# Queries and values of batch 0 and keys of batches 0 to 2, projected in the first stage and finished one half per expert block

## The chip, the cores and the metric

One core of one Trainium2 chip. The time is the device time of one execution in microseconds. PE is TensorE, DVE VectorE, ACT ScalarE, POOL GpSimd; SP issues DMAs only.

## The reference

```
xn  = layernorm(x)                       # x (4, 1024, 256), no scale or shift
q   = xn @ Wq + bq  -> 8 heads of 128    # k, v = xn @ Wkv + bkv, one head of 128 for all
q, k += sinusoidal positions             # (1024, 128)
s   = softmax(causal(q @ k.T / sqrt(128))) @ v @ Wo
g   = silu(moe(xn))   # 8 experts, top 2 of a softmax over router logits;
                      # relu(xn @ w1 + b1) @ w2 + b2, 256 -> 1024 -> 256
out = x + s * g
```

## The kernel before

Every matrix product is done in float16 halves: an operand is split into a high half (the value rounded to f16) and a low half (the rest), and three products (high by high, high by low, low by high: `PASSES`) are added in PSUM. So a projection of 128 columns of weights by 512 tokens, called a **job** here, is six matmuls of 512 columns (two chunks of 128 inputs by three passes); a job of values ("V") is 24 matmuls of 128. A query or key of 1024 tokens is two jobs. Each job is finished in steps: scale and add positions (DVE), add the bias and round to the high half (ACT), subtract for the low half (DVE).

**First stage** (`routing`). DVE, ACT and POOL normalise x (32 tiles of 128 rows) and split it; PE turns it; PE multiplies by the router's weights; DVE picks the two experts of each row (`choose`), PE counts (`counts`), DVE works out slots and one-hot rows (`one_hots`), and PE adds up, in eight groups of 8 matmuls (`place`), which token stands in each of 71 units of 128 rows. With that table (`who`) POOL gathers rows. POOL also splits the key/value weights and, of Wq, head 0 alone (L809 to L815). PE projects K and Q of head 0 of batch 0, four jobs (`project`, L482); ACT copies their banks to SBUF (L606), and one DMA puts them into DRAM (`kq_d`). ACT and DVE also split the weights of experts 0 and 1.

**Expert stage** (`experts`). 40 blocks, in the order `ORDER`: 22 of two units of 128 rows (twins), then 9 twins in turn with 9 of one unit. PE does `up` of block n between `down` of block n-1. Each block has four quarters q: ACT does the ReLU of quarter q (L1008) out of PSUM, DVE splits it (`split`: L1032 and L1034), PE's `down` of the next block's time reads it. DVE's `rows(n-2)` (L1044) stands between the splits of quarters 0 and 1. Behind the fourth ReLU, ACT's queue issues the transposing loads of block n+3 (L218), the store of the outputs of block n-2 (L996) and reads the next block's expert number. POOL gathers one unit and splits one piece of weights (512 columns) at a time (L261 to L265): experts 2 to 7, then Wq (4 pieces), then Wo (4 pieces); SP issues the loads. In blocks 30, 32, 34 and 36 (`KQ_AT`) one of the four early jobs is finished in a **round**: positions (L1061, DVE, behind the split of quarter 0), high half (L1014, ACT, behind the fourth ReLU), low half (L1065, DVE, in the next block behind the split of quarter 0).

**Attention** (`attention`). 32 heads n of five groups of score rows. PE does scores, values of the head before, and jobs given by the table `Jobs`: for step k = 5n+i the job that PE projects there.

```
if n == 0:
    job = (("Q", 1, 0), ("Q", 1, 1), ("V", 0, 0), ("V", 0, 1), ("Q", 2, 0))[i]
...
elif i in (0, 2) and n + 2 < heads:
    job = ("Q", n + 2, i // 2)
elif i == 1 and n % HEADS >= 4 and HEADS * (b + 1) < heads:
    job, bank = ("KKVV"[n % HEADS - 4], b + 1, n % 2), "S"
```

From head 9 on, the output tile of an earlier batch (`o_tile`, 24 matmuls of 256 columns) comes behind the fifth group. SP turns the probabilities by transposing DMAs (L1571).

## Time and profile before

| what | us |
| --- | --- |
| median of 3 runs (1076.97 to 1078.37) | 1077.34 |
| the profiled execution, its span | 1078.8 |
| PE busy / DVE busy / ACT busy / POOL busy | 990.9 / 857.8 / 641.9 / 336.8 |
| first matmul of the first expert block | 85.12 |
| end of the expert stage | 470.1 |
| first exponential of head 0 | 474.37 |

The profile gives the profiled execution's span and no other time of it, so the span stands for it. "Busy" is the time in which an engine has an instruction in it. In a timeline, a row is one or several instructions in a sequence: its start, its length, engine, source line, what it writes and reads, shapes, and in brackets the idle time of the engine before it and what ended it. ACTq is ACT's instruction queue: a DMA issue is in the queue and not on the engine. "<-issue" is idle time in which the engine waits for its own queue.

### The profile page before, as it was taken

How to read it: one execution, taken by the hardware profiler on the slowest of the kernel's cores; microseconds unless marked ns; L12 is line 12 of the kernel's file. 1: busy time of each engine (PE TensorE's matmuls, PEld its weight loads, DVE VectorE, ACT ScalarE, POOL GpSimd, SP SyncE). 2: the span in 40 equal slices, each digit the busy share in tenths (PEclk: the TensorE clock that was granted, in tenths of full speed). 3: DMA queues.
4: the chain of work that ended last, by engine and by line, in shares of the span. 5: the costliest groups of instructions: out<-in, count | busy, mean ns of one | idle time of the engine just before them, and what ended most of it. 6: DMA issues, size and time to landing. Idle time of an engine off the chain costs nothing.

```text
span 1078.8 us, 25081 instructions
## 1 busy us (share of the span) xinstructions
PE 990.9 (92%) x8686; PEld 778.5 (72%) x8686; DVE 857.8 (80%) x1535; ACT 641.9 (59%) x1358; POOL 336.8 (31%) x350
## 2 busy tenths in 40 slices
PE   0747999999999999998989889999999999999997
PEld 0536888888888898865656667767777677677776
DVE  6985776666766455569999999998999999999971
ACT  2722333233333333357888888878888878788860
POOL 3215999989995000020101002121212111112111
PEclk9968999999999999999999999999999999999999
DMA  8778666666666322149887879798999878888992
GB/s 273 211 287 182 157 181 177 174 179 184 171 172 147 95 60 65 46 121 159 171 154 141 157 142 186 152 164 150 172 189 178 150 150 162 153 171 160 181 179 95
DMA packets 410137, 172.58 MB, mean 160 GB/s; under 512 B 351994, under 2 KB 399940, under 8 KB 409252
## 3 DMA queue, kind: packets, MB, share of 16 engines
q1 hardware_dynamic: 352816, 129.80, 57.5%
q10 hardware_dynamic: 50724, 23.50, 8.6%
q0 software_dynamic: 6480, 17.70, 6.5%
q8 instruction: 77, 1.26, 0.5%
q14 instruction: 40, 0.33, 0.1%
HBM read 52.84 MB, written 31.72 MB: 78 GB/s over the span
## 4 chain that ended last, share of the span: by engine, by line
PE 37%; DVE 10%; DMA 5%; ACT 2%; issue 1%; SPq 0%; ACTq 0%; DVEq 0%
PE b_psO L1265 11%; PE b_psS L1242 11%; PE b_psJ L1281 5%; DMA b_pT<-b_ph 5%; PE b_psJ L1201 5%; DVE b_nmax L1426 3%; DVE b_ph L1462 3%; PE b_psS L1292 2%; PE b_psO L1267 1%; PE b_psS L1201 1%; DVE b_outs L1468 1%; ACT b_pr L1346 1%; ACT b_ph L1376 1%; PE b_psS L1245 1%; DVE b_Q L1449 1%
## 5 line engine op out<-in xcount | busy, mean ns | idle before, releaser
L933 PE MATMUL psU<-bxT,w_p 128*128 128x256 f16 (+1 forms) x1920 | 287.5, 262 | 13.3 <-DVE w_p L276 9.3
L1008 ACT ACTIVATE h<-psU,bias 128x256 f32<-128x256 f32 (+1 forms) x320 | 125.3, 448 | 273.6 <-PE psU L933 171.5
L942 PE MATMUL psY<-w_p,hp 128*128 x1704 | 273.4, 273 | 2.1 <-DVE hp L1034 2.1
L1242 PE MATMUL b_psS<-b_kp,b_Q 128*128 128x512 f16 (+3 forms) x1152 | 218.8, 326 | 1.5 <-PEq L1086 1.5
L1346 ACT ACTIVATE b_pr<-b_psS,b_nmax 128x1024 f32<-128x1024 f32 (+7 forms) x256 | 187.0, 735 | 47.9 <-DVE b_nmax L1426 27.1
L933 PEld LDWEIGHTS psU<-bxT,w_p 128*128 x1920 | 188.4, 98 | 34.0 <-issue 15.1
L1265 PE MATMUL b_psO<-b_pT,b_vp 128*128 128x256 f16 x1536 | 189.7, 274 | 20.3 <-issue 13.5
L1462 DVE SCALAR_TENSOR_TENSOR b_ph<-b_pr,b_rrec,b_ph 128x1024 f16<-128x1024 f32 (+7 forms) x256 | 199.4, 810 | 0.0
L1376 ACT ACTIVATE b_ph<-b_pr,b_rrec 128x1024 f16<-128x1024 f32 (+7 forms) x256 | 187.0, 768 | 15.4 <-DVE b_rrec L1455 14.1
L1032 DVE CAST hp<-h 128x512 f16<-128x512 f32 (+1 forms) x160 | 88.9, 556 | 133.7 <-ACT h L1008 127.5
L1426 DVE TENSOR_REDUCE b_nmax<-b_psS 128x1 f32<-128x1024 f32 (+7 forms) x256 | 183.1, 746 | 13.9 <-PE b_psS L1245 12.4
L942 PEld LDWEIGHTS psY<-w_p,hp 128*128 128x128 f16 x1704 | 166.1, 98 | 23.4 <-issue 3.5
L1265 PEld LDWEIGHTS b_psO<-b_pT,b_vp 128*128 128x128 f16 x1536 | 145.0, 98 | 44.1 <-issue 19.1
L1242 PEld LDWEIGHTS b_psS<-b_kp,b_Q 128*128 128x128 f16 x1152 | 103.2, 98 | 78.9 <-issue 2.2
L1539 POOL DMA_INDIRECT b_yg<-expert_outputs,pos x64 | 68.4, 1069 | 246.1 <-DMA expert_outputs<-y 119.5
L1545 POOL TENSOR_TENSOR b_x_row<-b_G,b_x_row 128x256 f32<-128x256 f32 x24 | 17.4, 727 | 368.6 <-DVE b_G L1489 359.8
L1034 DVE TENSOR_TENSOR hp<-h,hp 128x512 f16<-128x512 f32 (+1 forms) x160 | 127.1, 794 | 5.5
L179 POOL DMA_INDIRECT rowx<-xn_split,who x71 | 78.0, 1099 | 65.9 <-DVE who L796 43.4
L1281 PE MATMUL b_psJ<-b_wo,b_outs 128*128 128x256 f16 x576 | 66.9, 273 | 0.0
L265 POOL TENSOR_TENSOR w_p<-wstage,w_p 128x512 f16<-128x512 f32 x48 | 64.5, 1343 | 4.1
L1366 ACT ACTIVATE b_Q<-b_psJ,bias 128x512 f16<-128x512 f32 x59 | 40.6, 687 | 32.5 <-DVE b_psJ L1435 32.1
L1281 PEld LDWEIGHTS b_psJ<-b_wo,b_outs 128*128 128x128 f16 x576 | 55.2, 98 | 6.5
(187 smaller groups left out, 1027.1 us busy)
## 6 DMA issues: line engine op xcount, KB each, us to landing
wstage<-in_L_ffn_w SPq DMA_DIRECT2D x48, 256.0 KB
expert_rows<-rowx SPq DMA_DIRECT2D x67, 128.0 KB
expert_outputs<-y ACTq DMA_DIRECT2D x31, 256.0 KB
a_x_all<-in_L_attn_x SPq DMA_DIRECT2D x8, 512.0 KB, 9.7
...
```

The lines of the kernel that those rows point to most:

```text
L933: mm = eng.matmul(psU[w % U][:, g % 2, 0:tiles * P].rearrange("p (t r) -> p t r", t=tiles), weight(n, a * W1 + c * H + g * P, P), bxT[n % ...
L942: mm = eng.matmul(psY[n % 2][:, t, :], hp[n % 2][:, a, g, t * P:(t + 1) * P], weight(n, 2 * W1 + (2 * g + b) * D, D), start=(g == 0 and k ...
L1008: a = eng.activation(h32[w % 4][:, g, 0:rows], psU[w % U][:, g, 0:rows], ACT.Relu, bias=bias[:, ds(e * HT + 2 * q + g, 1)], scale=1.0 / WS)
L1032: eng.tensor_copy(hi, full).then_inc(hh_, 1)
L1034: eng.tensor_tensor(lo, full, hi, ALU.subtract).then_inc(hl_, 1)
L1242: mm = eng.matmul(dst, Q[n % 3][:, a, u * P:(u + 1) * P], kb[:, c, lo:lo + w], start=(kk == 0), stop=(kk == 2 and not last))
L1265: eng.matmul(both, vb[:, a, j, :], pT[:, at:at + hop + 1:hop, :], start=(j == 0 and kk == 0), stop=False)
L1281: mm = eng.matmul(psJ[:, 0:D], outs[b % many][:, a, h, t * P:(t + 1) * P], wo_p[:, e, h, :], start=(h == 0 and kk == 0), stop=(h == HEADS ...
L1346: a = eng.activation(pr[k % 3][:, o:o + w], psS[BUF[i]][:, :, :].rearrange("p a n -> p (a n)")[:, o:o + w], ACT.Exp, bias=nmax[:, at:at + ...
L1376: a = eng.activation(ph[k % 4][:, 2 * o:2 * o + w], pr[k % 3][:, o:o + w], ACT.Copy, scale=rrec[:, at:at + 1])
L1426: a = eng.tensor_reduce(nmax[:, at:at + 1], psS[BUF[i]][:, :, :].rearrange("p a n -> p (a n)")[:, o:o + w], AX.X, ALU.max, negate=True)
L1462: a = eng.scalar_tensor_tensor(ph[k % 4][:, 2 * o + w:2 * o + 2 * w], pr[k % 3][:, o:o + w], rrec[:, at:at + 1], ph[k % 4][:, 2 * o:2 * o ...
```

## The change

20 jobs more are projected in the first stage, 24 in all (`EARLY`: K0, Q0, V0, Q1 to Q7 of batch 0, K1, K2), two halves j of 512 tokens each; they are taken out of the table of attention. For that, POOL splits the whole of Wq in the first stage (it had come as four pieces in the expert stage), PE projects two jobs between the transposes, four ahead of `counts`, five behind it, one behind each of the first five groups of `place` and eight behind the last, in six PSUM banks; ACT copies each bank to SBUF. All of PE's and ACT's queues wait for the last copy ahead of block 0. In blocks 0 to 7 ACT's queue stores three raw jobs each to DRAM. In blocks 4 to 27 one job per block is finished, as round r = n - 4 (rounds 0 to 7 take jobs 16 to 23, rounds 8 to 23 jobs 0 to 15): positions behind DVE's third split, high behind ACT's fourth ReLU, the store of the halves of round r-1 and the load of round r+1 behind it, low half behind DVE's first split of the next block. The two jobs of V0 (rounds 12 and 13) have no positions. SP loads K0, Q0, V0 and Q1 at the end of its expert part; Q2 to Q7, K1 and K2 are loaded in attention, one per head.

The diff, cut to its core:

```diff
+EARLY = [("K", 0), ("Q", 0), ("V", 0)] + [("Q", h) for h in range(1, HEADS)] + [("K", 1), ("K", 2)]
+EARLY_JOBS = [(kind, m, j) for kind, m in EARLY for j in range(2)]
+NJ = len(EARLY_JOBS)
+JOBS_UP = 16
+ROUND_JOB = list(range(JOBS_UP, NJ)) + list(range(JOBS_UP))
...
-            if job:
+            if job and job not in EARLY_JOBS:
...
+            if e in (3, 4):
+                project(e - 3)
...
-        for r in range(3):
-            project(r)
+        for q in range(2, 6):
+            project(q)
         eng.wait_ge(s_bz, 3)
         counts()
-        project(3)
+        for q in range(6, 11):
+            project(q)
         for s in range(CHUNKS):
             place(s)
-        eng.wait_ge(s_kc, 4)
+            if s < 5:
+                project(11 + s)
+        for q in range(JOBS_UP, NJ):
+            project(q)
+        eng.wait_ge(kqc_, NJ)
...
         eng.wait_ge(xs_, 64)
-        for r in range(4):
-            eng.wait_ge(s_kp, r + 1)
-            eng.activation(kq_f[:, r, :], flat[r], ACT.Copy, scale=SC / WS).then_inc(s_kc, 1)
+        for q in range(NJ):
+            if q == JOBS_UP:
+                eng.wait_ge(s_sp, 1)
+            eng.wait_ge(s_kp, q + 1)
+            eng.activation(v["job_at"][q], job_bank[q % 6], ACT.Copy,
+                           scale=(1.0 if EARLY_JOBS[q][0] == "V" else SC) / WS).then_inc(kqc_, 1)
...
-        for i, (full, p) in enumerate(((wkv_f, wkv_p), (wq_f, wq_p))):
+        for i, (full, p) in enumerate(((wkv_f, wkv_p), (wq_f[:, :, 0:512], wq_h[:, :, :, 0:512]),
+                                       (wq_f[:, :, 512:], wq_h[:, :, :, 512:]))):
...
-        eng.dma_start(wq_f[:, :, :], wq[:, 0:HD].rearrange("(c p) n -> p c n", p=P)).then_inc(s_kw, 16)
+        eng.dma_start(wq_f[:, :, :], wq.rearrange("(c p) n -> p c n", p=P)).then_inc(s_qw, 16)
...
+        def load_raw(r):
+            eng.wait_ge(kqr_[r // 8], 128)
+            if r >= 2:
+                eng.wait_ge(kqb_, r - 1)
+            eng.dma_start(kq_t[r % 2][:, :], kq_d[ROUND_JOB[r]]).then_inc(kql_[r % 2], 16)
+
+        def high(r):
+            if r >= 2:
+                eng.wait_ge(kqs_[r % 2], 16 * (r // 2))
+            if EARLY_JOBS[ROUND_JOB[r]][0] == "V":
+                eng.wait_ge(kql_[r % 2], 16 * (r // 2 + 1))
+                eng.activation(kq_o[r % 2][:, 0], kq_t[r % 2][:, :], ACT.Copy).then_inc(kqa_, 1)
+            else:
+                eng.wait_ge(kqt_, summed(r))
+                eng.activation(kq_o[r % 2][:, 0], kq_t[r % 2][:, :], ACT.Identity, bias=column(r)).then_inc(kqa_, 1)
...
                 a.then_inc(rl_, 1)
-            if n in KQ_AT:
-                r = KQ_AT[n]
-                eng.wait_ge(kqt_, r + 1)
-                eng.activation(kq(r)[0][:, 0], kq_t[:, :], ACT.Identity, bias=kq(r)[1]).then_inc(kqa_, 1)
+            r = n - ROUND0
+            if 0 <= r < NJ:
+                high(r)
+            if 1 <= r <= NJ:
+                put_halves(r - 1)
+            if -1 <= r < NJ - 1:
+                load_raw(r + 1)
+            for i in range(PUT * n, min(PUT * n + PUT, NJ)):
+                put_raw(i)
             if n == 0:
                 v["load"](eng, 2)
...
+        def positions(r):
+            kind, m, j = EARLY_JOBS[ROUND_JOB[r]]
+            if kind != "V":
+                eng.wait_ge(v["pe_"], 16)
+                eng.wait_ge(kql_[r % 2], 16 * (r // 2 + 1))
+                eng.tensor_tensor(kq_t[r % 2][:, :], kq_t[r % 2][:, :], pe_sb[:, j * 512:(j + 1) * 512], ALU.add).then_inc(kqt_, 1)
...
                 split(n, q)
...
+                if q == 0 and 1 <= n - ROUND0 <= NJ:
+                    lower(n - ROUND0 - 1)
+                if q == 2 and 0 <= n - ROUND0 < NJ:
+                    positions(n - ROUND0)
```

**Where the order changes.** PE in the first stage, from the last logits to the first expert block, before (L489 is a projection, L511 a group of placing, L499 to L505 the counts):

```order
L476 MATMUL psU<-a_rw_p,a_xT 128x8 x48
L489 MATMUL psU<-xTb_next,wkv_p 128x512 x12
L489 MATMUL psU<-xTb_next,a_wq_p 128x512 x6
L499 MATMUL psU<-a_one_100,a_M_109 128x128 x2
L504 MATMUL psU<-a_tri_92,a_tot_93 128x264 x2
L505 MATMUL psU<-a_M_109,a_up_99 128x256
L489 MATMUL psU<-xTb_next,a_wq_p 128x512 x6
L511 MATMUL psU<-a_oh_q,a_oh_r 128x71 x64
L885 TENSOR_LOAD blk_e
```

and in the change (L508 and L504 are projections, L530 placing, L518 to L524 the counts):

```order
L523 MATMUL psU<-a_tri_98,a_tot_99 128x264 x2
L524 MATMUL psU<-a_M_115,a_up_105 128x256
L508 MATMUL psY<-xTb_next,wq_late 128x512 x12
L508 MATMUL psU<-xTb_next,wq_late 128x512 x18
L530 MATMUL psU<-a_oh_q,a_oh_r 128x71 x8
L508 MATMUL psU<-xTb_next,wq_late 128x512 x6
...
L530 MATMUL psU<-a_oh_q,a_oh_r 128x71 x24
L508 MATMUL psU<-xTb_next,wq_late 128x512 x12
L508 MATMUL psY<-xTb_next,wq_late 128x512 x12
L508 MATMUL psU<-a_xT,wkv_p 128x512 x24
L921 TENSOR_LOAD blk_e
```

Eight projections now stand between the last group of placing and block 0. ACT from the last ReLU of a block to the first of the next, in the expert stage, before:

```order
L1008 ACTIVATE h_3_132<-psU,bias 128x256
L218 DMA_TRANSPOSE bxT_67<-expert_rows 128x4x128 x2
L996 DMA expert_outputs<-y_72 128x2x256
L885 TENSOR_LOAD blk_e
L885 ISA x2
L1008 ISA
L1008 ACTIVATE h_0_129<-psU,bias 128x256
```

and in the change, in block 6:

```order
L1072 ACTIVATE h_3_137<-psU,bias 128x256
L1054 ACTIVATE kq_o_82<-kq_t_80,bias 128x512
L1059 DMA early_halves<-kq_o_83 256x1x512
L1044 DMA kq_t_81<-early_raw 128x512
L1038 DMA early_raw<-a_jobs_up 128x512 x3
L234 DMA_TRANSPOSE bxT_67<-expert_rows 128x4x128 x2
L1035 DMA expert_outputs<-y_72 128x2x256
L921 TENSOR_LOAD blk_e
L921 ISA x2
L1072 ISA
L1072 ACTIVATE h_0_134<-psU,bias 128x256
```

The high half (L1054) and its wait stand ahead of all that was behind the fourth ReLU. DVE in the change, one block of that kind (L1122 is positions, L1130 the low half):

```order
L1101 CAST hp_138<-h_2_136 128x512
L1103 TENSOR_TENSOR hp_138<-h_2_136,hp_138 128x512
L1122 TENSOR_TENSOR kq_t_80<-kq_t_80,pe_sb 128x512
L1101 CAST hp_138<-h_3_137 128x512
L1103 TENSOR_TENSOR hp_138<-h_3_137,hp_138 128x512
L1101 CAST hp_139<-h_0_134 128x512
L1103 TENSOR_TENSOR hp_139<-h_0_134,hp_139 128x512
L1130 SCALAR_TENSOR_TENSOR kq_o_82<-kq_t_80,bias,kq_o_82 128x512
L921 TENSOR_LOAD blk_e
```

Positions came in behind the third split, and the low half behind the first split of the block after.

## Rows read from the trace of the kernel before

**Rows 1.** Windows, by stage: length, busy us of each engine, granted clock, DMA share, GB/s
```profile
48.00:85.12 37.12, 17.47 (x98) 10.67 (x95) 33.69 (x89) 12.88 (x25) 5.91 (x6) 0.67 0.79 284
...
140.00:320.00 180.00, 180.00 (x1652) 161.33 (x1650) 122.13 (x154) 56.99 (x136) 164.69 (x172) 1.00 0.64 176
320.00:378.00 58.00, 55.83 (x569) 49.63 (x567) 31.10 (x59) 19.61 (x54) 19.21 (x21) 1.00 0.50 123
```

**Rows 2.** Windows of attention heads: 0, 1 to 5, 10, 12 and 13, 30
```profile
474.37:489.46 15.09, 14.58 (x122) 8.86 (x119) 14.25 (x26) 14.03 (x30) 4.67 (x5) 1.00 0.74 184
489.46:579.22 89.76, 78.82 (x598) 53.06 (x598) 85.72 (x153) 75.17 (x155) 9.47 (x10) 1.00 0.85 157
651.11:668.53 17.42, 17.42 (x141) 12.60 (x140) 16.69 (x31) 14.87 (x30) 2.99 (x3) 1.00 0.87 172
685.95:724.25 38.30, 38.30 (x295) 26.49 (x294) 35.77 (x65) 31.11 (x63) 5.89 (x6) 1.00 0.85 152
1013.88:1029.73 15.85, 15.50 (x136) 11.82 (x133) 14.34 (x27) 13.53 (x29) 2.95 (x3) 1.00 0.96 186
```

**Rows 3.** Timeline of PE, first stage: start, us, engine, line, shapes, idle before it
```profile
51.87 1.46 PE L489 MATMUL psU<-xTb_next,a_wq_p 128*128 128x512 f16 x6
...
64.35 1.26 PE L511 MATMUL psU<-a_oh_q,a_oh_r 128*128 128x71 f16 x8 [7.47 <-DVE a_oh_q L758]
...
74.53 1.26 PE L511 MATMUL psU<-a_oh_q,a_oh_r 128*128 128x71 f16 x8 [0.19 <-DVE a_oh_q L758]
85.12 7.55 PE L933 MATMUL psU<-bxT,w_p 128*128 128x256 f16 x54 [9.34 <-DVE w_p L276]
```

**Rows 4.** Timeline of ACT and its queue (ACTq) in two expert blocks
```profile
159.03 1.21 ACTq L218 DMA_TRANSPOSE bxT<-expert_rows  x1
...
200.95 1.30 ACTq L218 DMA_TRANSPOSE bxT<-expert_rows  x1
...
203.61 0.60 ACTq L996 DMA_DIRECT2D expert_outputs<-y  x1
204.96 0.84 ACT L1008 ACTIVATE h<-psU,bias 128x256 f32<-128x256 f32 x2 [3.36 <-issue]
```

**Rows 5.** Timeline of DVE in the same two blocks
```profile
169.49 1.53 DVE L1034 TENSOR_TENSOR hp<-h,hp 128x512 f16<-128x512 f32 x1
...
205.90 0.43 DVE L1032 CAST hp<-h 128x512 f16<-128x512 f32 x1 [2.77 <-ACT h L1008]
...
210.53 0.97 DVE L1034 TENSOR_TENSOR hp<-h,hp 128x512 f16<-128x512 f32 x1
...
212.84 0.69 DVE L1034 TENSOR_TENSOR hp<-h,hp 128x512 f16<-128x512 f32 x1
```

**Rows 6.** Timeline of PE in the block after
```profile
216.18 0.82 PE L942 MATMUL psY<-w_p,hp 128*128 x6
```

**Rows 7.** The rounds' operations at L1061 and L1065, ns min/median/max
```profile
L1061 DVE TENSOR_TENSOR kq_t<-kq_t,pe_sb x4: 684/684/685, 392.3 to 441.6; 128x512 f32<-128x512 f32 x4
...
L1065 DVE SCALAR_TENSOR_TENSOR b_Q<-kq_t,bias,b_Q x2: 744/745/746, 431.4 to 448.6; 128x512 f16<-128x512 f32 x2
```

**Rows 8.** Timeline of POOL, first stage
```profile
27.10 1.46 POOL L811 TENSOR_SCALAR a_wkv_f<-a_wkv_f 128x512 f32<-128x512 f32 x1
...
29.33 1.67 POOL L815 TENSOR_TENSOR wkv_p<-a_wkv_f,wkv_p 128x512 f16<-128x512 f32 x1
...
32.36 1.19 POOL L815 TENSOR_TENSOR a_wq_p<-a_wq_f,a_wq_p 128x256 f16<-128x256 f32 x1
```

**Rows 9.** Timeline of DVE, first stage, beside POOL and after it
```profile
28.00 1.39 DVE L651 TENSOR_SCALAR a_x_all<-a_x_all,a_mv,a_rs 128x256 f32<-128x256 f32 x2
...
32.34 1.75 DVE L657 TENSOR_TENSOR a_xp<-a_x_all,a_xp 128x512 f16<-128x512 f32 x2
...
35.27 0.73 DVE L651 TENSOR_SCALAR a_x_all<-a_x_all,a_mv,a_rs 128x256 f32<-128x256 f32 x2
35.91 0.68 DVE L657 TENSOR_TENSOR a_xp<-a_x_all,a_xp 128x512 f16<-128x512 f32 x1
```

More of the change, by code:

```diff
@@ L153, in build @@
     wq_late = top.take("wq_late", [P, 2 * DC * HEADS * HD], F16)
+    rounds = Arena(nc, top_at)
+    kq_t = [rounds.take(f"kq_t{i}", [P, 512], F32) for i in range(2)]
+    kq_o = [rounds.take(f"kq_o{i}", [P, 2, 512], F16) for i in range(2)]
+    given = Arena(nc, top_at)
+    vp0 = given.take("b_vp0", [P, 2, QT, HD], F16)
+    Q1 = given.take("b_Q1", [P, 2, T], F16)
+    assert rounds.at <= top_at + 2 * 2 * DC * T and given.at <= top_at + 2 * 2 * DC * T
     whole = ExitStack()
@@ L885, in expert, with summed, column @@
         return eng.value_load(blk_e[0:1, b:b + 1], min_val=0, max_val=E - 1)
-    def kq(r):
-        at = slice(r % 2 * 512, (r % 2 + 1) * 512)
-        return (kp0 if r < 2 else Q0)[:, :, at], bias[:, B_K:B_K + 1] if r < 2 else bias[:, B_Q:B_Q + 1], pe_sb[:, at]
+    def summed(r):
+        return sum(1 for i in range(r + 1) if EARLY_JOBS[ROUND_JOB[i]][0] != "V")
+    def column(r):
+        kind, m, j = EARLY_JOBS[ROUND_JOB[r]]
+        at = B_K if kind == "K" else B_Q + m % HEADS
+        return bias[:, at:at + 1]
     def on_sync(eng):
@@ L1176, in attention @@
         xl = [sem(f"xT_in{i}") for i in range(2)]
+        ql = [sem(f"Q_in{i}") for i in range(3)]
+        kl_ = sem("K_in")
         yl = [sem(f"y_in{i}") for i in range(3)]
@@ L1252, in values @@
                     eng.wait_ge(al_, 2 * (n - 1) + s // 2 + 1)
-                if n % HEADS == 0 and s == 0:
-                    eng.wait_ge(jl_, jobs.order.index(("Q", 2, 0)) + 1 if n == 0 else jobs.count("V", n // HEADS))
+                if n and n % HEADS == 0 and s == 0:
+                    eng.wait_ge(jl_, jobs.count("V", n // HEADS))
                 vb = vp[n // HEADS % many]
```

164 lines of the change are left out of this document (98 added, 66 removed).

## The prediction

> **What bounds the kernel now.** I read the views in this order: busy time by stage, then the queue of each engine in one expert block, then the attention heads one by one. The span is 1078.8 us. In the middle of the expert stage PE is busy for all of 180 us, with DVE at 122, ACT at 57 and POOL at 165 us [rows 1]: the blocks follow PE, 96 matmuls every 10.48 us (180 us for 1652 matmuls are 0.109 us each). From block 22 on, where blocks of two row tiles alternate with blocks of one, DVE is half idle and PE 2 us short of full [rows 1]. In attention PE and DVE share the bound. Head 10, with one query projection (two jobs) and an output tile, is PE throughout (17.42 of 17.42 us); heads 1 to 5 of batch 0 take 89.76 us with DVE busy 85.72 and PE 78.82 [rows 2]. So the change takes work from a place that is bound (heads 0 to 5, and heads 12 and 13) and puts its matmuls where PE waits for DVE (9 us ahead of the first block, 7.5 us ahead of placing the one-hot rows [rows 3]) and its finishing among expert blocks, where each engine but PE has idle time. Idle time is not room, though, if the added steps form a chain.
>
> **The chain in an expert block.** ACT's queue: after the last ReLU of a block it issues two transposes and a store, reads the next expert number, and only then comes the next block's first ReLU. From the first of these issues to that ReLU it is 4.0 us (200.95 to 204.96), and the profile calls the wait "issue" [rows 4]. DVE's queue: first split of the block 0.94 us after that ReLU began, row sums, second and third split; the third ends at 211.50 [rows 5], 10.55 us after ACT's first issue. The other pattern is the block 42 us earlier, 159.03 to 171.02, 11.99 us, where DVE's instructions beside a working POOL run longer (1.53 instead of 0.97 us) [rows 4, 5]. Twelve of the 17 full blocks from 4 on look like the first, five like the second: mean 10.9. Today nothing leads from the third split back to ACT's issues: they wait for the last ReLU, hence for PE, and the fourth split (ends 213.53) is ahead of the matmuls that read it (216.18 [rows 6]) by 2.6 us.
>
> The change closes this into a loop. In blocks 4 to 27 DVE adds the positions of round r after the third split, and ACT's high(r) waits for them, ahead of the halves' store, the next raw load, both transposes and the next block's ReLUs. Queued behind that wait are therefore the very ReLUs that the next positions need. One turn costs: 10.9 as above; two more DMA issues, 1.0 (one like the store's 0.60 [rows 4], one with half its rows, taken as 0.4); lower, 0.75, and positions, 0.68 [rows 7], less 0.08 of overlap each, 1.3; two hand-offs between engines near 0.1, where DVE begins 0.1 after ACT's second half ReLU ends [rows 4, 5]. Together 13.2 us, against PE's 10.48. Bounds: with the 10.55 pattern, short issues and no hand-off 12.6; with the 11.99 pattern 14.3. I take the mean. So PE, which never waited here, waits about 2.7 us in each.
>
> **The sum, part by part.**
> *First stage.* POOL now splits all of Wq: 2048 columns a partition instead of 256. The 512 of Wkv take 3.9 us (27.10 to 31.00), the 256 took 2.6, to 33.55 [rows 8], so 15.6 less 2.6, 13.0 us more of POOL beside DVE's normalising. Beside POOL, four DVE groups from 28.00 to 34.1 took 6.3 us (first 1.39, last 1.75), which without it take 4.0 (0.73 and 1.29, twice; one pass of L657 is 0.68) [rows 9]: 2.3 lost in 6.4 us of POOL, 0.36 of it. That gives +4.7; the bounds are 0 (POOL waits instead) and 13.0 (DVE stands still), and 4.7 is nearest to the row. The Trainium skill says more (SBUF — State Buffer, Who interferes with whom): when one of the two holds the shared port, the other "fully blocks". By this rule for every instruction the delay would be the whole 13.0; in this trace single DVE instructions wait and others run at full length beside POOL, so the trace bears it out in part.
> Placing: eight groups of 1.26 us, one per 1.45 of DVE, last at 74.53 [rows 3]; five projections are put between them. At full clock (2.4 GHz) a projection is 1.3 us (1.46 [rows 3] less the last one's drain). If placing is 0.7 at full clock, a pair lasts 2.0, five pairs 10 and three groups 2.1, 1.0 more than today's 11.4. At the half clock (1.2 GHz) to which the granted clock fell there (0.67 in the mean over the stretch [rows 1]) it would be 5 more or worse. I take +1.0, since six projections and copies now fill the 7.5 us of idling in which the clock fell. Behind placing come eight projections, 10.4, and a last copy, 0.5, before either queue may enter block 0. So block 0 begins at 75.8+4.7+1.0+10.4+0.5 = 92.4 instead of 85.12: +7.3. Its 54 matmuls took 7.55 [rows 3] where the later cadence gives 5.9: −1.6. **First stage +5.7** (+2 to +14). The row gathers end well before 92; the copies lie beside PE and cost nothing else.
> *Expert stage.* The rounds of blocks 4 to 21: rounds 12 and 13 (values) have no positions, which breaks the loop, so there are 15 turns: 15 times 2.7 is 40.5. Three raw stores of 0.37 (again half the store's rows, here at the short end) more on ACT in blocks 4 to 7: 4.4. Less 2 for PE's slack, used up at the first round and again after the value rounds. Blocks 22 to 27: a pair takes about 17 us; the turns of 2.3 twice add 4.6, of which something is covered: 3 pairs by 4, +12 (0 to 15). The four rounds of today vanish: −1. **Expert stage +54** (+29 to +72). The four Wq pieces go from POOL, which is ahead of PE anyhow: 0. The 24 raw stores, loads and halves put at most five times 0.26 MB into a block, 124 GB/s beside 176 [rows 1]; waits for landings I count at 0, hidden by a load issued one whole block ahead.
> *Attention.* Head 0 loses five jobs; it took 15.09, DVE busy 14.25 [rows 2]. Without some 5 us of DVE work, ACT's exponentials and halves bound it near 13: −2. Heads 1 to 5 lose 13 jobs: the nearest row without jobs is head 30, 15.85, with an output tile that they lack [rows 2]; its DVE is busy 14.34. Between 14.0 and 15.85 I take 15.3, since ACT (13.5), DVE and PE hand over to each other: 76.5 instead of 89.76, −13.3. Heads 12 and 13 become like head 10: 34.8 instead of 38.30, −3.5. Each of heads 1 to 5 now loads 0.5 MB beside a DMA share of 0.85, in head 30 even 0.96 [rows 2]: +1. **Attention −17.8** (−21 to −10).
> In all +5.7+54−17.8 = +42: 1120.7 us in a profile. The profiled execution stands 1.5 us above the median of 1077.34, so the time is **1119**.
>
> **Rivals.**
> (a) The rounds are hidden. If high(r) does not hold up ACT's next ReLUs (positions come early, or PE's lead covers it), the expert stage costs 1 instead of 54: 1066, **faster**. For it: DVE has 58 of 180 us free, ACT 123 [rows 1], and the four rounds of today cost almost nothing. Against it: those add positions behind the first split, when ACT is still in its ReLUs. It decides at the turn's length: below 10.48 us no PE time is lost; I know no reading below 12.
> (b) DVE stands still for POOL in the first stage: +8.3, 1127. The Trainium skill's rule above would lead here.
> (c) Transfers run late: the DMA share in these blocks is 0.64 before anything is added [rows 1], and in blocks 4 to 7 the raw load may land after the third split. Two to four us more in eight blocks and a crowded head 1 to 5: 1137.
> (d) The loop holds but is shorter, 12 us (no contention, issues dispatched early): 15 times 1.5 and pairs at 2: 1094.
>
> **How the numbers follow.** Forecast 0.58, (a) 0.10, (b) 0.08, (c) 0.12, (d) 0.12. A change of 0.2% (2.2 us) can just be told. The range 1090 to 1141 leaves out (a) and the far tail of (c); the bounds of the loop (12.6 to 14.3) alone move the time by −9 to +17. Only (a) is faster: 0.10; the same, if it is half true, 0.02; slower 0.88.
>
> **What the profile would show.** Right: in blocks 5 to 21 PE idle some 2.7 us a block, released by DVE's subtraction, cadence near 13; ACT idle before high, released by positions; block 0 near 92; heads 1 to 5 near 15.3; heads 12, 13 at 17.4. Wrong: PE full in blocks 4 to 21; then rival (a), and the error is in the order of the waits. If positions wait for a raw load, it is (c). If placing runs at half clock or DVE's normalising ends past 53 us, the first stage was underpriced.

## The result and the profile of the changed kernel

The changed kernel takes **1155.18 us** (median of 4 runs, 1150.26 to 1157.6) where the kernel before took 1077.86 (4 runs, 1076.97 to 1078.66): a ratio of **1.0695, 95% interval 1.0654 to 1.0737**, +77 us. The forecast was slower, 1119, with 1141 as its upper end. The direction came as said, and so did the loop in the expert blocks; the size did not, and the five attention heads that were to give most of the gain gave none. The sections below find which terms were too small. A ratio in this document leaves out executions more than 1.5% above the fastest of their kernel, which concerns one of the twelve of f3.

All line numbers of the profile after are those of the changed file: L1122 adds the positions, L1130 is lower, L1054 high, L1059 stores the halves, L1044 loads and L1038 stores the raw projections, L1072 is ReLU, L1101 and L1103 split, L1113 sums the rows, L234 and L1035 are ACT's transposing loads and store, L972 and L981 the matmuls up and down, L508 and L504 the projections, L530 placing.

First the windows by stage. The cuts are the first ReLU of block 0, 4, 8, 16, 22 and 28, then the first exponential; columns as in [rows 1]. The kernel before, cut at the same blocks:

```profile
87.90:131.40 43.50, 40.14 (x358) 34.33 (x357) 27.27 (x34) 13.10 (x32) 30.76 (x33) 1.00 0.71 168
131.40:173.30 41.90, 41.90 (x387) 37.55 (x385) 29.70 (x36) 13.50 (x32) 38.58 (x41) 1.00 0.65 181
173.30:257.20 83.90, 83.90 (x771) 75.21 (x769) 55.23 (x72) 26.73 (x64) 76.03 (x82) 1.00 0.62 177
257.20:320.30 63.10, 63.10 (x580) 56.56 (x579) 43.72 (x54) 20.18 (x48) 58.16 (x60) 1.00 0.66 175
320.30:374.30 54.00, 51.83 (x532) 46.02 (x531) 28.74 (x54) 17.14 (x48) 18.99 (x20) 1.00 0.53 129
374.30:474.37 100.07, 98.07 (x1010) 86.61 (x1008) 55.69 (x119) 37.03 (x100) 1.02 (x2) 1.00 0.22 61
```

The changed kernel, the same blocks:

```profile
102.00:147.60 45.60, 42.80 (x384) 36.59 (x382) 26.12 (x34) 12.88 (x32) 34.96 (x38) 1.00 1.01 245
...
147.60:211.20 63.60, 50.54 (x420) 41.51 (x419) 35.63 (x43) 15.23 (x36) 54.54 (x57) 0.95 0.81 225
211.20:326.60 115.40, 91.08 (x753) 73.82 (x752) 75.82 (x88) 30.40 (x72) 102.82 (x106) 0.96 0.80 197
326.60:395.40 68.80, 64.06 (x569) 55.92 (x567) 39.49 (x64) 22.88 (x54) 21.54 (x22) 0.98 0.62 162
395.40:458.30 62.90, 54.90 (x527) 47.26 (x525) 31.08 (x66) 20.50 (x54) 0.00 (x0) 0.95 0.33 89
458.30:558.90 100.60, 96.10 (x988) 85.06 (x986) 52.08 (x112) 34.21 (x97) 1.00 (x2) 0.98 0.27 76
```

Line by line the blocks lose 2.1, 21.7, 31.5, 5.7, 8.9 and 0.5 us, 70.4 together. Blocks 8 to 15 are the plainest: 14.4 us each instead of 10.5, with PE busy for 91 of 115 us. POOL is busy for 103 of them, but its work is not what sets the pace: in e1 below the same blocks take 88 us. Who waits for what there (blocks 8 to 15; us in total, times, longest):

```profile
ACT kq_o L1054 <- DVE kq_t L1122: 44.6, 8, 6.3
DVE hp L1101 <- ACT h L1072: 40.7, 8, 7.2
```

Each engine waits for the other, once a block, 5.6 and 5.1 us each time: that is how a loop looks. One turn of it, on ACT and its queue:

```profile
249.64 0.72 ACT L1054 ACTIVATE kq_o<-kq_t,bias 128x512 f16<-128x512 f32 x1 [5.19 <-DVE kq_t L1122]
249.66 0.55 ACTq L1059 DMA_DIRECT2D early_halves<-kq_o  x1
250.31 0.56 ACTq L1044 DMA_DIRECT2D kq_t<-early_raw  x1
250.97 2.66 ACTq L234 DMA_TRANSPOSE bxT<-expert_rows  x2
253.66 0.59 ACTq L1035 DMA_DIRECT2D expert_outputs<-y  x1
255.33 1.93 ACT L1072 ACTIVATE h<-psU,bias 128x256 f32<-128x256 f32 x5 [4.97 <-PE psU L972]
```

and on DVE, up to the positions for which ACT waits next:

```profile
256.27 0.48 DVE L1101 CAST hp<-h 128x512 f16<-128x512 f32 x1 [4.42 <-ACT h L1072]
256.79 0.98 DVE L1103 TENSOR_TENSOR hp<-h,hp 128x512 f16<-128x512 f32 x1
257.69 1.09 DVE L1130 SCALAR_TENSOR_TENSOR kq_o<-kq_t,bias,kq_o 128x512 f16<-128x512 f32 x1
258.71 0.68 DVE L1113 SCALAR_TENSOR_TENSOR y<-psY,b2b 128x512 f32<-128x512 f32 x1
...
261.25 0.97 DVE L1103 TENSOR_TENSOR hp<-h,hp 128x512 f16<-128x512 f32 x1
262.15 1.09 DVE L1122 TENSOR_TENSOR kq_t<-kq_t,pe_sb 128x512 f32<-128x512 f32 x1
```

From 249.54, where the positions before ended, 0.1 us ahead of high, to 263.24 it is 13.7 us: 5.8 to the ReLU, 0.9 to the first split, 7.0 to the end of the positions. ACT's wait for PE in the last line of ACT's list (4.97) is no contradiction: PE's matmuls for that ReLU had been done for 8 us, and the issues held it back, as in [rows 4].

The first stage, PE's timeline, and below it the row of DVE that takes the counts:

```profile
53.72 5.28 PE L508 MATMUL psU<-xTb_next,wq_late 128*128 128x512 f16 x12
...
61.58 0.28 PE L518 MATMUL psU<-a_one,a_M 128*128 128x128 f16 x2
...
71.71 1.27 PE L530 MATMUL psU<-a_oh_q,a_oh_r 128*128 128x71 f16 x8 [1.68 <-DVE a_oh_q L787]
72.81 2.74 PE L508 MATMUL psU<-xTb_next,wq_late 128*128 128x512 f16 x6
75.34 1.24 PE L530 MATMUL psU<-a_oh_q,a_oh_r 128*128 128x71 f16 x8
76.40 1.48 PE L508 MATMUL psY<-xTb_next,wq_late 128*128 128x512 f16 x6
...
87.94 2.77 PE L508 MATMUL psU<-xTb_next,wq_late 128*128 128x512 f16 x12
...
100.42 0.84 PE L972 MATMUL psU<-bxT,w_p 128*128 128x256 f16 x6 [1.94 <-DVE w_p L286]
```
```profile
61.89 0.42 DVE L816 CAST a_tot<-psU 128x256 f16<-128x256 f32 x1 [1.98 <-PE psU L518]
```

Block 0 begins at 100.42 instead of 85.12 [rows 3]: +15.3, where 92.4 was forecast. Placing begins 7.4 us later. Of this, 5.7 us are DVE's, whose choice of experts (`a_M`) was ready at 59.8 instead of 54.1 us. The other 1.7 are PE's: the four projections ahead of the counts ran until 61.6, at a mean granted clock of 0.66, and DVE waited 1.98 us for the counts behind them. Placing then takes 16.2 us, up to the first projection behind it, instead of 11.4.

Attention: head 0, heads 1 to 5, heads 12 and 13, head 30 (columns as in [rows 2]):

```profile
558.90:572.35 13.45, 7.11 (x47) 3.60 (x44) 9.96 (x19) 11.85 (x25) 4.69 (x5) 1.00 0.96 270
572.35:662.09 89.74, 73.46 (x531) 50.63 (x532) 70.25 (x126) 67.65 (x141) 9.47 (x10) 0.89 0.97 188
...
766.57:801.41 34.84, 34.84 (x281) 25.22 (x280) 33.38 (x61) 29.73 (x61) 5.97 (x6) 1.00 0.88 167
1090.55:1106.39 15.84, 15.44 (x135) 11.65 (x132) 14.33 (x27) 13.53 (x28) 2.95 (x3) 1.00 1.00 186
```

Heads 12 and 13 give the 3.5 us, head 0 gives 1.6. Heads 1 to 5 give nothing: 89.74 us against 89.76 [rows 2], though DVE is busy for 70 instead of 86 us. The granted clock fell from 1.00 to 0.89 there. In each of these heads PE's timeline shows one long wait, of 3.0 to 3.7 us, and behind it one slow group of 21 matmuls, of 3.7 to 4.6 us. Two of the five:

```profile
591.23 4.12 PE L1354 MATMUL b_psO<-b_pT,b_vp 128*128 128x256 f16 x21 [3.66 <-DMA b_pT<-b_ph]
...
608.77 4.00 PE L1354 MATMUL b_psO<-b_pT,b_vp 128*128 128x256 f16 x21 [3.34 <-issue]
```

Attention as a whole, to the last instruction, gained 7.5 us (604.4 to 596.9). That is 2.4 more than heads 0, 12 and 13 give, and probably no effect of the change: heads 9 and 25, whose work is unchanged, took 18.7 and 18.8 us in the trace before and 17.2 and 17.4 here. Such long heads come in other places in the traces of f3 (9, 17, 24 and 26) and e3 (26). With +15.3 at the front and the blocks' +69.2, counted here from block 0's first matmul, this makes the 77.

### The profile page after: what moved, and what is told of

It reads as the page before. It is cut to its first block, busy times and chain, and to the rows that moved or that the text cites. A ratio compares the mean times of both kernels' runs of the same rounds, so it can differ in the third digit from the quotient of the medians.

```text
span 1155.8 us, 25243 instructions
## 1 busy us (share of the span) xinstructions
PE 1019.6 (88%) x8686; PEld 784.9 (68%) x8686; DVE 860.9 (74%) x1535; ACT 650.3 (56%) x1378; POOL 335.0 (29%) x341
## 4 chain that ended last, share of the span: by engine, by line
PE 35%; DVE 8%; ACT 3%; DMA 2%; issue 2%; SPq 0%; ACTq 0%; DVEq 0%
PE b_psO L1354 11%; PE b_psS L1331 10%; PE b_psJ L1370 5%; PE b_psJ L1285 4%; DVE b_nmax L1515 3%; DMA b_pT<-b_ph 2%; DVE b_ph L1551 2%; ACT b_pr L1435 2%; PE b_psS L1381 2%; PE b_psO L1356 1%; DVE b_outs L1557 1%; PE b_psS L1334 1%; PE b_psS L1285 1%; ACT b_ph L1465 1%; ACT b_outs L1443 1%
## 5 line engine op out<-in xcount | busy, mean ns | idle before, releaser
L972 PE MATMUL psU<-bxT,w_p 128*128 128x256 f16 (+1 forms) x1920 | 296.2, 266 | 46.0 <-issue 34.8
L981 PE MATMUL psY<-w_p,hp 128*128 x1704 | 282.5, 279 | 11.9 <-DVE hp L1103 11.8
L1072 ACT ACTIVATE h<-psU,bias 128x256 f32<-128x256 f32 (+1 forms) x320 | 119.2, 456 | 231.4 <-PE psU L972 136.3
L972 PEld LDWEIGHTS psU<-bxT,w_p 128*128 x1920 | 189.5, 100 | 75.6 <-issue 55.1
L1101 DVE CAST hp<-h 128x512 f16<-128x512 f32 (+1 forms) x160 | 83.1, 519 | 186.4 <-ACT h L1072 180.6
L1354 PE MATMUL b_psO<-b_pT,b_vp 128*128 128x256 f16 x1536 | 196.6, 280 | 25.9 <-DMA b_pT<-b_ph 13.5
L981 PEld LDWEIGHTS psY<-w_p,hp 128*128 128x128 f16 x1704 | 168.5, 100 | 40.7 <-issue 16.7
L1354 PEld LDWEIGHTS b_psO<-b_pT,b_vp 128*128 128x128 f16 x1536 | 148.2, 100 | 53.0 <-issue 23.8
L1103 DVE TENSOR_TENSOR hp<-h,hp 128x512 f16<-128x512 f32 (+1 forms) x160 | 120.5, 753 | 5.5
L1285 PE MATMUL b_psJ<-b_xTb,wq_late 128*128 128x512 f16 x288 | 70.0, 379 | 0.0
L1054 ACT ACTIVATE kq_o<-kq_t,bias 128x512 f16<-128x512 f32 x22 | 15.9, 722 | 86.0 <-DVE kq_t L1122 86.0
L275 POOL TENSOR_TENSOR w_p<-wstage,w_p 128x512 f16<-128x512 f32 x48 | 61.9, 1289 | 4.1
```

Of the source, the lines that this page charges most:

```text
L972: mm = eng.matmul(psU[w % U][:, g % 2, 0:tiles * P].rearrange("p (t r) -> p t r", t=tiles), weight(n, a * W1 + c * H + g * P, P), bxT[n % ...
L981: mm = eng.matmul(psY[n % 2][:, t, :], hp[n % 2][:, a, g, t * P:(t + 1) * P], weight(n, 2 * W1 + (2 * g + b) * D, D), start=(g == 0 and k ...
L1072: a = eng.activation(h32[w % 4][:, g, 0:rows], psU[w % U][:, g, 0:rows], ACT.Relu, bias=bias[:, ds(e * HT + 2 * q + g, 1)], scale=1.0 / WS)
L1103: eng.tensor_tensor(lo, full, hi, ALU.subtract).then_inc(hl_, 1)
L1285: mm = eng.matmul(out, lhs(a, c), rhs(b, c), start=(k == 0), stop=(k == 3 * DC - 1))
L1354: eng.matmul(both, vb[:, a, j, :], pT[:, at:at + hop + 1:hop, :], start=(j == 0 and kk == 0), stop=False)
```

## The experiments

### Is it the loop? Three ways to open it

**e1: positions earlier.** One condition in DVE's program:

```
-                if q == 2 and 0 <= n - ROUND0 < NJ:
+                if q == 0 and 0 <= n - ROUND0 < NJ:
                     positions(n - ROUND0)
```

> The changed kernel with one row of the program moved: DVE adds the positions of round r behind the first split of the block instead of behind the third. Work, transfers and ACT's queue stay. Theory L (the loop third split, positions, high, issues, next ReLU sets blocks 4 to 27): high finds its input ready, blocks 8 to 15 fall from 14.5 us to 10.5 to 11.5, and the time from 1155 to 1100 to 1115. Rival T (the raw load or the transfers in general are late, rival (c) of the prediction): positions now wait for the load, the blocks stay over 13.5 and the time at 1145 or more. Rival W (the added work and issues as such fill ACT's and DVE's queues, wherever they stand): blocks of 12.5 to 13.5, the time 1125 to 1140.

Measured: 1109.4 us. **e2** is the same edit with `q == 1`:

> As the run before, but the positions stand behind the second split. Theory L: the turn is shorter by about one split (some 2 us of the 14.5), so blocks 8 to 15 at 12 to 12.8 and the time 1120 to 1135, between the two. Rivals T and W: within 5 us of the run with the positions behind the first split.

Measured: 1125.2 us. **e9** leaves DVE alone and changes ACT's order:

```
-            r = n - ROUND0
-            if 0 <= r < NJ:
-                high(r)
-            if 1 <= r <= NJ:
-                put_halves(r - 1)
-            if -1 <= r < NJ - 1:
-                load_raw(r + 1)
...
             if n >= 2:
                 store(n - 2)
+            r = n - ROUND0
+            if 0 <= r < NJ:
+                high(r)
+            if 1 <= r <= NJ:
+                put_halves(r - 1)
+            if -1 <= r < NJ - 1:
+                load_raw(r + 1)
```

> The changed kernel with DVE's order left alone (positions behind the third split) and ACT's order changed: raw stores, the two transposes and the store of outputs stand ahead of high, the halves' store and the raw load, so ACT issues them while it would only wait for the positions. Theory L (the loop runs through ACT's issues): some 2.5 to 3 us of issues leave the turn, blocks 8 to 15 fall from 14.5 to 11.3 to 12.3, the time from 1155 to 1108 to 1122. Rival V (it is DVE's order alone: positions and lower push the third and fourth split back): blocks 8 to 15 stay over 13.5, the time over 1142.

Measured: 1109.7 us. Blocks 8 to 15 in windows, first of e1, then of e2, then of e9:

```profile
195.00:282.70 87.70, 85.63 (x762) 72.45 (x760) 76.19 (x88) 30.87 (x72) 79.29 (x80) 1.00 0.80 217
```
```profile
205.50:306.10 100.60, 87.64 (x753) 71.55 (x751) 74.60 (x88) 31.08 (x72) 90.94 (x93) 0.99 0.81 207
```
```profile
193.90:284.70 90.80, 85.41 (x765) 73.32 (x763) 76.56 (x88) 31.71 (x72) 81.88 (x80) 1.00 0.76 211
```

A block takes 11.0, 12.6 and 11.4 us, against 14.4 with the loop and 10.5 before. Work, transfers and the number of waits are the same in all; only the length of the turn differs. In e1 ACT's waits for the positions are gone from the list of these blocks. In e9 they are 11.9 us instead of 44.6; another 13.2 us ahead of high stand as "issue", the DMA issues that now come first.

Theory L holds in the place where the two engines' orders cross, from either side; T falls (a raw load that was late would have made e1 worse than e2), V and W fall as main causes. The loop costs 46 of the 77 us. Of W a rest remains: e1's blocks 8 to 15 are 3.8 us longer in all than before's, with DVE busy for 76 of 88 us instead of 55 of 84.

### Blocks 4 to 7: the raw stores

**e5** takes e1 and moves the 24 raw stores from ACT's queue to SP's:

```
-            for i in range(PUT * n, min(PUT * n + PUT, NJ)):
-                put_raw(i)
...
+        eng.wait_ge(kqc_, NJ)
         for n in range(AHEAD + 4, UNITS):
+            for i in range(2 * (n - AHEAD - 4), min(2 * (n - AHEAD - 4) + 2, NJ)):
+                eng.dma_start(kq_d[ROUND_JOB[i]], v["job_at"][ROUND_JOB[i]]).then_inc(kqr_[i // 8], 16)
             v["keep"](eng, n)
```

> The kernel with positions behind the first split (e1_first_split, 1109.4 us), and the 24 stores of raw projections issued by SP, two per row tile that it keeps, instead of by ACT, three per block. Theory A (blocks 4 to 7 are longer than 8 to 15 because ACT's own queue is filled by issues: ACT's ReLU waited 13.1 us for 'issue' between 145 and 195 us there): blocks 4 to 7 fall from 12.5 us in the mean to 11.0 to 11.5, the time by 4 to 7. Rival M (the memory traffic of these blocks, DMA share 1.03 against 0.65 before, holds up row tiles or staging, whoever issues): blocks 4 to 7 stay over 12, the time within 2.

Measured: 1105.9 us, blocks 4 to 7 in 45.5 us (11.4 each) instead of 49.7 (12.4), with the same DMA share. e1's blocks 4 to 7, then e5's:

```profile
145.30:195.00 49.70, 44.79 (x389) 37.85 (x387) 34.29 (x43) 15.33 (x36) 41.12 (x42) 0.97 1.03 260
```
```profile
143.90:189.40 45.50, 44.58 (x403) 38.72 (x401) 32.77 (x43) 15.33 (x36) 34.35 (x37) 1.00 0.99 263
```

So A holds in the blocks: the issues on ACT's queue cost 4.2 us there, not the traffic. The time shows less of it: 3.5 us below e1, instead of 4 to 7, and the ratios to the kernel before are 1.0274 and 1.0264, a difference that two runs each can't tell. A new wait took part of the gain: between 276 and 320 us PE waited once, 5.0 us, for POOL's expert weights, which we meet again below.

### The first stage

**e4** makes POOL wait for DVE's last split row before it begins on Wq:

```
             if i == 1:
                 eng.wait_ge(s_qw, 16)
+                low_done(eng, TWOS - 1)
```

> The changed kernel, with POOL holding back its six instructions on Wq until DVE has split the last normalised rows. Theory P (POOL beside DVE delays the normalising, and DVE the rest of the first stage): DVE's last low ends near 44 instead of 49.4, the counts 5 us sooner, the first block at 95 to 97 instead of 100.4, unless the projections of Q, which now get their weights later, take that back. Rival C (the delay of DVE is covered, what counts is PE's own length at the granted clock): the first block stays within 1.5 us of 100.4.

DVE's last low, in the changed kernel and then in e4:

```profile
50.36 0.69 DVE L686 TENSOR_TENSOR a_xp<-a_x_all,a_xp 128x512 f16<-128x512 f32 x1 [0.28 <-ACT a_xp L572]
```
```profile
43.95 0.69 DVE L686 TENSOR_TENSOR a_xp<-a_x_all,a_xp 128x512 f16<-128x512 f32 x1 [0.28 <-ACT a_xp L572]
```

It comes 6.4 us sooner (44.37 in the kernel before), and block 0 begins at 95.83 instead of 100.42. P holds. Of the 6.4 us 4.6 arrive; on the way stand POOL's work, now beside DVE's selection of experts (one of its operations took 2.23 us), and a projection that waited 2.0 us for its weights. The time, 1153.2 (2 runs, 1147.67 and 1158.77), shows little of it, since those runs spread by more than the effect; the place in the trace decides.

The slow DVE groups themselves, beside POOL's six instructions on Wq (30.01 to 40.26), in the changed kernel, and the same two kinds of group right behind them:

```profile
30.10 2.96 DVE L686 TENSOR_TENSOR a_xp<-a_x_all,a_xp 128x512 f16<-128x512 f32 x2
32.99 3.26 DVE L680 TENSOR_SCALAR a_x_all<-a_x_all,a_mv,a_rs 128x256 f32<-128x256 f32 x2
...
40.66 0.68 DVE L686 TENSOR_TENSOR a_xp<-a_x_all,a_xp 128x512 f16<-128x512 f32 x1
41.26 0.73 DVE L680 TENSOR_SCALAR a_x_all<-a_x_all,a_mv,a_rs 128x256 f32<-128x256 f32 x2
```

**e7** puts the five projections behind placing instead of between its groups:

```
         for s in range(CHUNKS):
             place(s)
-            if s < 5:
-                project(11 + s)
-        for q in range(JOBS_UP, NJ):
+        for q in range(11, NJ):
             project(q)
```

> The changed kernel with the five projections that stand between the eight groups of placing put behind them. Theory S (placing and projections add up on PE, with about 1.1 us a group even at the full clock): placing goes at DVE's pace, 1.45 us a group, ends near 83 instead of 88, and 13 projections instead of 8 follow; the first block begins at 100 to 103 instead of 100.4. Rival H (the interleaving itself is dear, because the clock falls in it and each group waits for a projection that started just before): the first block begins at 96 to 98.5.

Block 0 began at 101.47: theory S. Interleaving is not dear in itself: with DVE's pace between the groups (1.45 us each) and 13 projections behind them, the sum comes out 1 us longer. The time, 1152.5 (1148.6 and 1156.3), is no difference that two runs can tell.

### Heads 1 to 5

**e3** leaves out the loads of the queries of heads 3 to 7 from HBM, and the waits for them:

```
-                if i == 1 and 1 <= n < HEADS - 2:
-                    early_in(("Q", n + 2), Q[(n + 2) % 3], ql[(n + 2) % 3])
```

> The changed kernel without the five loads of the queries of heads 3 to 7 (0.5 MB each; these heads compute with the queries of heads 0 to 2, which leaves the loads out and changes no instruction count of PE, DVE or ACT). Theory D (heads 1 to 5 gained nothing because the added loads crowd the turned probabilities on the DMA engines and in SP's queue): heads 1 to 5 fall from 89.7 us to 78 to 82, the time by 8 to 14. Rival O (the order of the hand-offs, transposes and their latency, set these heads whether or not Q is loaded): heads 1 to 5 stay within 3 us of 89.7.

The five heads:

```profile
566.95:657.13 90.18, 73.51 (x530) 50.96 (x531) 70.22 (x126) 67.75 (x141) 9.45 (x10) 0.89 0.86 158
```

The DMA share fell from 0.97 to 0.86, the heads stayed at 90.2 us. Theory D is dead; rival O's number came, which e6 tests further. (The time, 1150.3, is 5 us lower, of which the first stage has 2.5 and the blocks the rest; nothing of it lies in attention.)

**e6** fills PE's wait with twelve matmuls that nobody reads:

```
+                    if 1 <= n < HEADS - 2 and i == 1:
+                        for _ in range(2):
+                            proj(psJ[:, :], lambda a, c: kp[0][:, a, c * P:(c + 1) * P],
+                                 lambda b, c: kp[0][:, b, c * 512:(c + 1) * 512])
                     if n and i:
                         values(n - 1, i - 1)
```

> The changed kernel, with twelve more matmuls of 512 columns (2.6 us at the full clock) in each of heads 1 to 5, put where PE waits 3.3 to 3.7 us for the turned probabilities ahead of the values; their result is read by nobody, so nothing of the kernel's work is changed. Theory K (without jobs PE idles there, the granted clock falls to 0.5 and the 21 matmuls behind take 4.0 to 4.1 us instead of 2.3, which is what makes the head as long as with its jobs): the clock of heads 1 to 5 rises from 0.83 to 0.91 to 0.97 or more, each head falls from 17.4 or more to 15.6 to 16.4, the five from 89.7 to 78 to 82, the time by 7 to 11. Rival O (the period is set by the order of hand-offs, maxima to turned probabilities, whatever PE's clock): the five heads stay at 87 or more.

The five heads, and in the second of them the group that had taken 4.12 us:

```profile
574.23:656.39 82.16, 74.98 (x578) 50.44 (x575) 70.52 (x126) 67.86 (x140) 9.47 (x10) 1.00 1.12 202
```
```profile
591.72 2.46 PE L1354 MATMUL b_psO<-b_pT,b_vp 128*128 128x256 f16 x21
```

82.2 us instead of 89.7, at a granted clock of 1.00: theory K. More work made the heads shorter. Per head 1.6 us come from the 21 matmuls themselves (3.7 to 4.6 us before, 2.46 now), enough for the whole difference. What the clock does not explain is the rest of the way to the forecast: at the full clock a head still takes 16.4 us, where 15.3 was said. The time did not follow, 1154.3: the expert stage was 2 us longer in this run, and later heads gave some back: heads 6, 16 and 28 took 18.5 to 18.9 us instead of 17.2 to 17.7. Such heads stand in other traces too (head 25 of the kernel before took 18.8); in heads 16 and 28 here PE waited once, 1.3 us, for turned probabilities. The other kernel with the filler, e8 below, has the same three long, 18.3 to 18.9 us. Why stays open.

### All of it together

> Positions behind the first split, raw stores on SP, POOL's work on Wq held back until DVE has normalised, filler matmuls in heads 1 to 5: what the theories L, P, A and K say together. From 1155: loop -46, POOL -4, stores -5, filler -9 gives 1091, between 1085 and 1100. Before is 1078: if all is as said the whole idea stays 0.7 to 2% behind, for the first stage's 8 late projections (10 us) and the slower cadence of blocks 4 to 27.

Measured: 1106.3 us (4 runs, 1097.37 to 1108.06), ratio 1.0244 with the interval 1.0168 to 1.0321. Not 1091: it is no better than e5. Block 0 began 2.8 us sooner than in e5 (96.48) and heads 1 to 5 took 81.9 instead of 88.2 us, but the blocks were 4.5 us longer than in e5, 2.3 of them because PE waited 7.3 us instead of 5.0 for POOL's weights between 276 and 310 us, and attention as a whole was only 0.7 us shorter than in e5: heads 6, 11, 13, 16 and 28 took 18.2 to 18.9 us where e5 has 17.2 to 17.7. Each effect has its place in a trace, yet they do not add up.

### The part of the idea that pays

What the runs say can be used the other way round: take from the change only what meets idle time and closes no loop. Heads 14, 15, 22 and 23 are PE throughout and carry one projection of values each. **f1** starts from the kernel before and projects only the values of batches 2 and 3 early, two projections ahead of placing and two behind it, and finishes them at once, without positions and without rounds:

```
+        for q in range(V_FIRST):
+            project_v(q)
         for s in range(CHUNKS):
             place(s)
+        for q in range(V_FIRST, 2 * len(V_EARLY)):
+            project_v(q)
...
+        for q in range(2 * len(V_EARLY)):
+            eng.wait_ge(s_kp, 5 + q)
+            eng.activation(v_f[:, q, :], v_bank[q], ACT.Copy, scale=1.0 / WS).then_inc(s_kc, 1)
+            eng.wait_ge(s_kc, 5 + q)
+            eng.activation(v_o[:, q // 2, 0, q % 2 * 512:(q % 2 + 1) * 512], v_f[:, q, :], ACT.Copy).then_inc(v["vh_"], 1)
```

The last five lines are ACT's, behind its copies of keys and queries. POOL subtracts the low halves, two ahead of its first gathers and two behind the gather of row tile 11; SP stores each batch's halves and loads them in heads 9 and 17. **f2** has V_EARLY = (1, 2, 3), with three projections on either side of placing.

> The kernel before, with only the values of batches 2 and 3 projected in the first stage: two of the four projections where PE waits 7.5 us ahead of placing, two behind placing where it waits 9.3 us. ACT copies them, ACT and POOL finish them there (POOL idle from 33.6 to 76.9 us), the halves go to HBM and come back in heads 9 and 17; there are no rounds in the expert blocks. Theory F (idle time of the first stage can be filled where nothing is chained to it, and a job less in a head that PE bounds saves 1.55 us, as heads 12 and 13 did): heads 14, 15, 22 and 23 fall from 18.97 to 17.4, -6.2, and the first block begins within 1 us of 85.1: 1070 to 1074 against 1077.8. Rival G (POOL or ACT late in the first stage holds up gathers or ReLUs, or the projections run at half clock and past 85 us): the first block or block 1 is 3 to 6 us later, the time within 2 of before or above.

> As f1_values23, with the values of batch 1 too: three projections ahead of placing and three behind, heads 6 and 7 lose their job too. Theory F: heads 6 and 7 fall from 18.0 to 17.1 to 17.4, 1 to 2 us more gained than f1_values23, unless three projections ahead of placing no longer fit into 7.5 us. Rival G: the first block is 1 to 3 us later than in f1_values23 and the gain is given back.

Measured: f1 1084.06 us (10 runs; ratio 1.0038, 1.0009 to 1.0067), f2 1092.62 (ratio 1.0122, 1.0078 to 1.0167). Both are slower than the kernel before, by less than 2%, though the heads did as expected: in f1 heads 14 and 15 took 34.4 us instead of 37.95. Where f1's gain went stands in one line of its PE timeline:

```profile
279.11 1.46 PE L976 MATMUL psU<-bxT,w_p 128*128 128x256 f16 x6 [5.38 <-POOL w_p L269]
```

POOL waited for the values' store before its first piece of expert weights, and began it at 110.58 instead of 104.44:

```profile
109.58 0.96 POOL L183 DMA_INDIRECT rowx<-xn_split,who  x1 [10.78 <-DMA early_values<-a_v_o]
110.58 0.73 POOL L265 TENSOR_SCALAR wstage<-wstage 128x512 f32<-128x512 f32 x1
```

Six us lost on POOL at 104 came out as 5.4 us on PE, which waited until 279: POOL, which the prediction called ahead of PE anyhow, has no slack in that expert. The first block began 0.9 us later, at 86.02. This accounts for the profiled execution, at 1080.7 us one of f1's faster ones; why its median lies 3 us higher no trace shows. Nor is f2's loss explained: the one profiled is its fastest (1084.35, with a wait of 3.3 us of the same kind), and the other three took 1090.9 to 1095.0. **f3** lets POOL wait for the store only ahead of the piece that overwrites the halves, and SP stores them some row tiles later. POOL's part of the edit:

```
-        eng.wait_ge(v["vs_"], 16 * len(V_EARLY))
         for n in range(AHEAD + 4, UNITS):
             v["gather"](eng, n)
+            if p == 5 * PIECES:
+                eng.wait_ge(v["vs_"], 16 * len(V_EARLY))
```

> f1_values23 with POOL no longer held for the values' store ahead of its first piece of expert weights (it waits for it only ahead of the piece that overwrites the halves), and SP storing them some row tiles later. In f1_values23 heads 14, 15, 22 and 23 took 17.1 to 17.4 us as expected, but POOL began its first piece at 110.6 instead of 104.4 us, and PE waited 5.4 us for w_p at 283 us. Theory H (these are one thing: POOL has no slack to lose there): POOL begins near 104.5, the wait at 283 goes, and the time falls by 5 to 7 to 1071 to 1075 where before has 1077 to 1080: faster by 0.4 to 0.7%. Rival I (the wait for w_p comes from something else, the DMA engines or POOL's pace beside DVE): PE still waits 3 us or more there and the time stays within 0.3% of before or above.

POOL's first piece, and heads 14 and 15, in f3:

```profile
101.07 0.64 POOL L265 TENSOR_SCALAR wstage<-wstage 128x512 f32<-128x512 f32 x1
```
```profile
723.09:757.60 34.51, 34.51 (x280) 25.07 (x279) 33.24 (x61) 29.61 (x61) 5.88 (x7) 1.00 0.87 169
```

Measured: **1076.96 us against 1079.72 (12 and 17 runs), ratio 0.9965, interval 0.9943 to 0.9987**. There is no wait of PE between 262 and 306 us any more: theory H. This version is faster than the kernel before by 0.35%, less than the 0.4 to 0.7% expected and half of the 0.6% that four heads by 1.6 us would give, and the changed kernel's 77 us are gone. The gain is at the limit of what these runs can tell: they lie between 1072.39 and 1088.54, those of the kernel before between 1076.75 and 1086.61, and with all twelve the ratio of the means is 0.9973 with an upper end of 1.000. In its first stage two of DVE's one-hot operations take 1.42 and 1.29 us instead of 0.45 beside POOL's two low halves (68.40 to 71.35), and PE waits 2.0 us for them; moving the low halves was not tried.

## Why the prediction was right and wrong

In the profile the change costs 77.0 us, 35.1 more than the forecast's 42. The first stage has 8.4 of these (14.1 instead of 5.7, up to the first ReLU), the expert blocks 16.4 (70.4 instead of 54), attention 10.3 (-7.5 instead of -17.8).

- **The loop** was right in place, order and kind: positions release high, high holds up the next ReLUs, and the blocks from 4 to 27 pay. e1, e2 and e9 show it. Rival (a) is out, and (c) too.
- **The length of a turn failed, as a term of the sum.** "Together 13.2 us" is 14.4 in blocks 8 to 15. The forecast took positions and lower from [rows 7], 0.68 and 0.75, measured at 392 to 449 us, when POOL no longer worked. In blocks 8 to 15 POOL works, and positions took 1.09 to 1.64 us (median 1.48), lower 1.09 in the median: 1.1 us more a turn. That is not the whole balance. Seven turns, from one high to the next, take 14.55 us in the mean. From the start of high to the ReLU it is 5.7 us, where 4.0 and 1.0 were said: the two added issues take 1.3 with the gaps between them, and in two turns a store or a pair of transposes took 0.5 to 1.5 us more than usual. From the first split to the end of the positions it is 7.8, where 5.9 and 1.3 were said: the 1.1 us more, less 0.5 by which splits and row sums were shorter than before. So half of the error is on ACT's queue, and half is that an operation was priced by a row from another stage, when [rows 5] already showed the same engine slower beside POOL. When POOL has finished, from block 18 to 22, the turns are 12.2, 12.0, 10.1 and 11.5, all shorter than forecast. Eight blocks by 1.2 us: +10.
- **Blocks 4 to 7** were forecast at 15.2 us more and cost 21.7: the same 1.2 us a block, and raw stores. Three issues of 0.37 us were said; the trace has 0.46 to 0.48 in the median, and up to 1.96 for the same instruction. e5 shows that issues on ACT's queue matter there. Blocks 0 to 3, which issue raw stores too, were put at nothing and cost 2.1.
- **Blocks 16 to 27** cost 14.6 us; the three turns of 16 to 21, the slack and the 12 us for pairs made 18. Blocks 28 on cost 0.5 where -1 was said.
- **The first stage** was to cost 5.7 us and cost 14.1. On DVE the delay, "+4.7", was about 6 (the last split ends 6.0 us later than before, and 6.4 later than in e4), but it came near by two errors that offset each other. POOL's work on Wq was put at 15.6 us and took 10.3; all of its work beside DVE's normalising grew by 6.6 us and not by 13.0. And the share of it that DVE loses was put at 0.36 and was 0.66: four groups took 10.9 us instead of 4.0 beside those 10.3 us. With the right length and the share of the forecast it would have been 2.4. By the Trainium skill (SBUF — State Buffer, Who interferes with whom) the loser fully blocks, which beside 10.3 us of POOL would be a loss of 10.3 (an estimate); the trace agrees in part, DVE lost 6.9. Rival (b)'s +8.3 would have met the 14.1, but by luck: most of what was missing came from three other terms.
- **The first stage, on PE.** Four projections ahead of the counts were put at nothing and held them up by 1.7 us, at a granted clock of 0.66. "If placing is 0.7 at full clock" was another: a group takes 1.06 us even at the full clock, and the first projection between them ran at a granted clock of 0.50 (2.74 us), so placing was 4.8 us longer and not 1.0. The eight projections behind it took 10.5, as said. The last copy and hand-over took 1.9 and not 0.5.
- **Heads 1 to 5** were to give 13.3 us and gave none. "ACT, DVE and PE hand over to each other: 15.3" failed as the path of a head: it left out what PE does when it waits. The granted clock over the group behind the wait is 0.57, so mostly 1.2 GHz, and the group takes 3.7 to 4.6 us instead of 2.46. Head 30, the row I leaned on, has its output tile (2.8 us) ahead of the scores before that place and no wait there, and its clock is 1.00. e3 excludes the loads, and e6 shows that the clock is 7.5 of the 13.3 us. The other 5.7, a head of 16.4 and not 15.3 at the full clock, stay open.
- **Heads 0, 12 and 13** came as forecast (-1.6 and -3.5 for -2 and -3.5). The 2.4 us more that attention gained are luck as far as the traces tell, by the long heads named above.

The range was too narrow for one reason more: its bounds on the turn (12.6 to 14.3), on the first stage (to +14) and on attention (to -10) were each nearly reached or passed at the unfavourable end. With the three parts at their upper bounds (+14, +72, -10) the sum is 1153, while the stated range ended at 1141. Three of the four missed terms have POOL or PE's clock in them.
